# Gathering token rows by a slot-to-token map in a mixture of experts, with three products of rounded halves

## What is computed

```python
x = x3.reshape(-1, h)                       # 800 tokens, h = 256
probs = jax.nn.softmax(x @ Wg, axis=-1)     # 8 experts
vals, idx = jax.lax.top_k(probs, 2)
weights = vals / (jnp.sum(vals, axis=-1, keepdims=True) + EPS)
cw = zeros((T, E)).at[arange(T)[:, None], idx].set(weights)
act = silu(einsum('th,ehf->tef', x, W1) + b1)        # f = 1024
y = einsum('tef,efh->teh', act, W2) + b2
out = einsum('te,teh->th', cw, y)
shared = silu(x @ Ws1 + bs1) @ Ws2 + bs2
out = out + 0.1 * shared
```

## Time and profile before

| What | us |
|---|---|
| Median of 3 runs | 1086.58 (1086.11 to 1089.01) |
| The profiled execution | 1087.61 |
| Its span, first to last instruction | 1085.5 |
| Mean granted TensorE clock | 0.958 of full speed |
| PE busy | 992.4 (91%) |
| DVE busy | 809.2 (75%) |
| ACT busy | 748.4 (69%) |
| POOL busy | 626.2 (58%) |

### The profile page before, as it was taken

The page is one execution under the profiler, slowest core; times in us unless marked ns, Lnnn a source line. Parts: engine busy times, 40 slices in busy tenths (PEclk is TensorE's granted clock), DMA queues, the critical chain, the costliest instruction groups (busy, mean ns, idle before and its releaser), DMA issues.

```text
span 1085.5 us, 16818 instructions
## 1 busy us (share of the span) xinstructions
PE 992.4 (91%) x5808; PEld 688.4 (63%) x5808; DVE 809.2 (75%) x954; ACT 748.4 (69%) x1722; POOL 626.2 (58%) x388
## 2 busy tenths in 40 slices
PE   5994898988999999899998998898999899999996
PEld 3543555655656556565665666676777665899995
DVE  7797999999999999999999998577666630211110
ACT  4999998999999999999999932556556532233221
POOL 2001999999999999999999956311110005022122
PEclk9995899999999999999999999799899899999998
DMA  5001344444444434344444414501000009599994
GB/s 194 9 8 51 102 112 113 109 112 111 113 112 109 112 110 113 112 110 113 107 112 111 112 38 143 149 15 29 2 2 2 1 1 365 152 292 320 319 304 123
DMA packets 91118, 125.44 MB, mean 116 GB/s; under 512 B 11641, under 2 KB 84490, under 8 KB 91018
## 3 DMA queue, kind: packets, MB, share of 16 engines
q1 hardware_dynamic: 87130, 120.04, 38.6%
q0 software_dynamic: 3904, 4.33, 2.1%
HBM read 115.93 MB, written 9.23 MB: 115 GB/s over the span
## 4 chain that ended last, share of the span: by engine, by line
PE 49%; DVE 28%; issue 12%; ACT 6%; DMA 2%; POOL 1%; DVEq 0%; POOLq 0%; ACTq 0%
DVE states L1791 15%; PE ps L1233 14%; PE ps L1580 7%; PE ps L1594 6%; DVE states L1769 4%; PE ps L1213 4%; PE ps L1108 3%; PE ps L1366 3%; PE ps L1378 2%; PE ps L1125 2%; DVE neg_max L1907 2%; ACT probs L1030 2%; POOL rows_by_slot L796 1%; PE ps L1394 1%; PE ps L1515 1%
## 5 line engine op out<-in xcount | busy, mean ns | idle before, releaser
L705 POOL TENSOR_TENSOR states<-states,c_row 128x800 f32<-128x800 f32 x255 | 472.8, 1900 | 89.6 <-DVE states L1791 89.4
L1233 PE MATMUL ps<-states,ident 128*128 128x400 f32 x1024 | 381.1, 508 | 11.4 <-DVE u L1799 11.4
L1233 PEld LDWEIGHTS ps<-states,ident 128*128 128x128 f32 x1024 | 186.9, 192 | 116.7 <-DVE u L1799 12.7
L1791 DVE TENSOR_TENSOR_SCAN states<-sb_decay,ps 128x800 f32<-128x800 f32 x128 | 231.5, 1808 | 4.8 <-ACT sb_decay L944 3.9
L1791 DVE TENSOR_TENSOR_SCAN states<-ps,states 128x800 f32<-128x800 f32 x128 | 229.8, 1795 | 1.1 <-ACT ps L944 1.1
L936 ACT ACTIVATE xT<-xn_tok,xT 100x256 f32<-100x256 f32 x512 | 216.4, 493 | 0.7 <-PE ps L1213 0.2
L944 ACT ACTIVATE ps<-dt,neg_a 128x396 f32<-128x396 f32 x256 | 141.2, 583 | 45.1 <-DVE states L1791 44.2
L1213 PEld LDWEIGHTS ps<-ident,xT 100*128 100x128 f32 x1024 | 101.1, 145 | 81.2 <-issue 62.6
L944 ACT ACTIVATE sb_decay<-dt,neg_a 128x396 f32<-128x396 f32 x256 | 144.4, 611 | 1.0 <-DVE states L1791 0.9
L1213 PE MATMUL ps<-ident,xT 100*128 100x100 f32 x1024 | 114.9, 257 | 29.4 <-DVE states L1791 17.6
L1030 ACT ACTIVATE probs<-ps,neg_max 100x361 f32<-100x361 f32 x128 | 70.8, 560 | 65.0 <-DVE neg_max L1907 64.5
(11 more groups left out here) (233 smaller groups left out, 1258.7 us busy)
## 6 DMA issues: line engine op xcount, KB each, us to landing
c_row<-rows SPq DMA_DIRECT2D x256, 200.0 KB, 3.1
w_tile<-in_w SPq DMA_DIRECT2D x40, 1024.0 KB, 8.0
b_row<-rows SPq DMA_DIRECT2D x32, 200.0 KB, 3.1
ctx<-in_ctxT SPq DMA_DIRECT2D x8, 361.0 KB, 4.2
rows_by_slot<-blank_rows SPq DMA_DIRECT2D x1, 2660.0 KB, 11.6
x_tile<-rows_by_slot SPq DMA_DIRECT2D x20, 133.0 KB, 3.3
win<-in_winT SPq DMA_DIRECT2D x2, 1024.0 KB, 10.8
w_shared<-in_w SPq DMA_DIRECT2D x2, 1024.0 KB, 6.8
```

Of the source, the lines that this page charges most:

```text
L705: nc.gpsimd.tensor_tensor(st, st, c_row[i % C_SLOTS][:].unsqueeze(1).broadcast_to([P, CP, TQ]), ALU.mult).then_inc(product_ready, 1)
L1233: mm = nc.tensor.matmul(ps[:, j, 0:TQ], ident[:], states[i % RING][:, j * TQ:(j + 1) * TQ], start=(n == 0), stop=(n == N - 1), skip_group_ ...
L1791: nc.vector.tensor_tensor_scan(st, rates, inflows, 0.0, ALU.mult, ALU.add).then_inc(scan_done, 1)
```

## The change

Rows by a map. DVE no longer sends slots to POOL. `places` (new) turns each pick's slot into a one-hot tile (20 columns) and a one-hot place (128 columns) in bf16, and `tokens` on PE, at unit 10, multiplies them in 16 matmuls of 40 columns, so that each slot receives the number of its token. `token_numbers` on DVE turns the sums into indices (blank slots get the numbers of blank rows). The token rows, without the number, are stored in DRAM once, by one plain DMA (`token_rows`), and POOL gathers each tile's 128 rows from it with one indirect DMA (`fetch`): two after unit 12, three after the shared expert, and from there one behind each addition. The 16 scatters, their blank rows and SP's `load_rows` go; the waits of SP's weight loads stay, but the second load waits for the split of the second weights instead of `tile_done`.

Three products. The shared expert's weights are split by POOL during the attention (two passes for each of two 128x2048 blocks, ahead of the third context's split). The inputs are split by ACT and DVE (first half) and ACT and POOL (second half), the hidden values by ACT (rounded copy) and POOL (what is left) in four slots. For the tiles, ACT makes the rounded copy of the hidden values in two halves and of the second weights (`high_second`), and DVE makes the low parts (`low_hid`, `low_second`). The tiles' first product stays float32.

Ranks. The picks' sum, the counting matrices and the ones are bf16, and `ranks` comes at unit 5. DVE computes the owners of the tiles (`experts_ready`) before the slots.

The diff, cut:

```diff
-SECOND_HALF_AT, LOGITS_AT, RANKS_AT, ROWS_AT = 1, 2, 6, 13
+SECOND_HALF_AT, LOGITS_AT, SPLIT_AT, RANKS_AT, INVERT_AT, FETCH_AT, ROWS_AT = 1, 2, 3, 5, 10, 12, 13
-SHARED_LAG = 2
-ROUTE_CONSTS = 13
+SHARED_LAG, HIDDEN_SLOTS, FETCHED_EARLY = 2, 4, 2
+ROUTE_CONSTS = 16
@@ sp
                 if turn > 0:
-                    sp.wait_ge(tile_done, turn)
+                    sp.wait_ge(second_split, turn)
                 load_second(w_tile[r], e, w2_in[r])
-            def load_rows(k):
...
-                    sp.wait_ge(tile_added, 16 * (k - X_SLOTS + 1))
-                sp.dma_start(x_tile[r][:], rows_by_slot[k * P:(k + 1) * P]).then_inc(rows_in[r], 16)
+            sp.wait_ge(cw_ready, 1)
+            sp.wait_ge(xn_ready, (1 + DIRS + 2) * B)
+            sp.dma_start(token_rows[FIRST_ROW:FIRST_ROW + T].rearrange("(b l) w -> l b w", l=L), rows_src[:]
+                         ).then_inc(token_rows_stored, 16)
@@ pool
+            for n, cols in enumerate((slice(W1_AT, W2_AT), slice(W2_AT, B1_AT))):
+                split_into([part[:, cols] for part in shared_part], shared_raw[:, cols], shared_split, 2 * n)
             split_context(2, 0, 2)
...
-            for j in range(PICKS):
-                for b in range(B):
-                    at = bass.IndirectOffsetOnAxis(ap=slot_idx[:, j * B + b:j * B + b + 1], axis=0)
-                    nc.gpsimd.indirect_dma_start(rows_by_slot, at, rows_src[:, b, :], None).then_inc(scattered, 16)
+            def low_hidden(u):
+                high, low = hidden_part[u % HIDDEN_SLOTS]
+                pool.wait_ge(hidden_high, u + 1)
+                nc.gpsimd.tensor_tensor(low[:], hidden_raw[u % HIDDEN_SLOTS][:], high[:].bitcast(F32), ALU.subtract
+                                        ).then_inc(hidden_split, 1)
...
+            def fetch(k):
+                r = k % X_SLOTS
+                if k >= X_SLOTS:
+                    pool.wait_ge(tile_taken, k - X_SLOTS + 1)
+                    pool.wait_ge(tile_weighed, k - X_SLOTS + 1)
+                at = bass.IndirectOffsetOnAxis(ap=token_of[:, k:k + 1], axis=0)
+                nc.gpsimd.indirect_dma_start(x_tile[r][:], None, token_rows, at).then_inc(rows_in[r], 16)
+            for u in range(UNITS):
+                low_hidden(u)
+                if u == SPLIT_AT:
+                    for k in range(KD):
+                        low_inputs(k)
+                if u == FETCH_AT:
...
+                    for k in range(FETCHED_EARLY):
+                        fetch(k)
...
                 nc.gpsimd.indirect_dma_start(sums, at, y_tile[k % 2][:], None, compute_op=ALU.add
                                              ).then_inc(tile_added, 16)
+                if k + X_SLOTS < TILES:
+                    fetch(k + X_SLOTS)
@@ act, a shared unit
+                nc.scalar.activation(raw[:], ps[:, u % 2, 0:TQ], ACT.Silu,
+                                     bias=b1_shared[:, ft:ft + 1]).then_inc(silu_done, 1)
+                act.wait_ge(silu_done, u + 1)
+                nc.scalar.activation(hidden_part[u % HIDDEN_SLOTS][0][:], raw[:], ACT.Copy).then_inc(hidden_high, 1)
@@ act, a tile
+            def high_second(k):
+                act.wait_ge(w2_in[k % W_SLOTS], 16 * (k // W_SLOTS + 1))
...
+                    act.wait_ge(tile_done, k - 1)
+                nc.scalar.activation(second_part[k % 2][0], w_tile[k % W_SLOTS][:, W2_AT:B1_AT], ACT.Copy
+                                     ).then_inc(second_high, 1)
...
+                    if ft % 4 == 3:
+                        half = slice(ft - 3, ft + 1)
+                        act.wait_ge(tile_silu, FT * k + ft + 1)
+                        nc.scalar.activation(high[:, half, :], raw[:, half, :], ACT.Copy).then_inc(hid_high, 1)
+                if k + 1 < TILES:
+                    high_second(k + 1)
@@ pe
+            def tokens():
+                pe.wait_ge(places_ready, 1)
+                for j in range(PICKS * B):
+                    mm = nc.tensor.matmul(ps[:, TOKEN_BANK, 0:2 * TILES], hot_place[:, j, :], by_tile[:, j, :],
+                                          start=(j == 0), stop=(j == PICKS * B - 1))
...
             def shared_second(u):
-                pe.wait_ge(silu_done, u + 1)
+                pe.wait_ge(hidden_split, u + 1)
                 for m in range(KD):
...
+                    mm = three(ps[:, 4 + 2 * q + m, 0:TQ], [part[:, at:at + P] for part in shared_part],
+                               [part[:] for part in hidden_part[u % HIDDEN_SLOTS]], ft == 0, False)
@@ pe, out_of_tile
-                pe.wait_ge(w2_in[k % W_SLOTS], 16 * (k // W_SLOTS + 1))
+                pe.wait_ge(second_split, k + 1)
                 for ft in range(FT):
+                    if ft % 4 == 0:
+                        pe.wait_ge(hid_split, 2 * k + ft // 4 + 1)
+                    mm = three(ps[:, 6 + k % 2, 0:D], [part[:, ft, :] for part in hid_part[k % 2]],
+                               [part[:, ft * D:(ft + 1) * D] for part in second_part[k % 2]], ft == 0, ft == FT - 1)
@@ dve
+            def places():
+                picked = PICKS * B
+                step(nc.vector.tensor_tensor(hot_tile[:], slot_sum[:].unsqueeze(2).broadcast_to([L, picked, TILES]),
...
+                nc.vector.tensor_tensor(hot_place[:], place_in[:].unsqueeze(2).broadcast_to([L, picked, P]),
+                                        place_no[:].unsqueeze(1).broadcast_to([L, picked, P]), ALU.is_equal
+                                        ).then_inc(places_ready, 1)
...
+            def low_hid(k, half):
+                dve.wait_ge(hid_high, 2 * k + half + 1)
...
+            def low_second(k):
+                dve.wait_ge(second_high, k + 1)
+                high, low = second_part[k % 2]
+                nc.vector.tensor_tensor(low, w_tile[k % W_SLOTS][:, W2_AT:B1_AT], high.bitcast(F32), ALU.subtract
+                                        ).then_inc(second_split, 1)
...
             for k in range(TILES):
+                for half in range(2):
+                    low_hid(k, half)
                 if k + 2 < TILES:
                     take_tile(k + 2)
+                if k + 1 < TILES:
+                    low_second(k + 1)
                 weigh_tile(k)
```

More of the change, by code:

```diff
@@ L311, in decoder_layer, with in_place @@
         moe = ExitStack()
[L312 removed]
+        def in_place(name, shape):
+            with ExitStack() as first:
+                raw = sb(f"{name}_raw", shape, scope=first)
+            return raw, sb(f"{name}_low", shape, F32R, scope=moe)
+        shared_raw, shared_low = in_place("shared", [P, B1_AT])
+        b1_shared = sb("b1_shared", [P, FT], scope=moe)
         rows_src = sb("rows_src", [L, B, RW], scope=moe)
@@ L716, in split_into @@
                 high, low = part
-                nc.gpsimd.tensor_tensor(high, raw, one[:].unsqueeze(2).broadcast_to(raw.shape), ALU.mult
-                                        ).then_inc(done, 1)
+                ones_of = one[:].unsqueeze(2) if len(raw.shape) == 3 else one[:]
+                nc.gpsimd.tensor_tensor(high, raw, ones_of.broadcast_to(raw.shape), ALU.mult).then_inc(done, 1)
                 pool.wait_ge(done, count + 1)
@@ L1060, in _ @@
             for k in range(KD):
+                job_result(act, ("xn3T", k, 0))
+                nc.scalar.activation(xn3_part[0][:, k, chunk(0)], bank(("xn3T", k, 0))[:, 0:TQ], ACT.Copy
+                                     ).then_inc(xn3_high, 1)
+            for k in range(KD):
+                act.wait_ge(xn3_low[0], k + 1)
                 copy_out(("xn3T", k, 0), xn3T[:, k, chunk(0)], bank(("xn3T", k, 0))[:, 0:TQ])
@@ L1072, in _ @@
                     nc.scalar.activation(route["exp"][:], route["shifted"][:], ACT.Exp).then_inc(exp_ready, 1)
+                if u == SPLIT_AT:
+                    for k in range(KD):
+                        job_copied(act, ("xn3T", k, 1))
+                        nc.scalar.activation(xn3_part[0][:, k, chunk(1)], xn3T[:, k, chunk(1)], ACT.Copy
+                                             ).then_inc(xn3_high, 1)
                 if u == ROWS_AT:
@@ L1508, in shared_first @@
                 if ft == 0:
-                    for k in range(KD):
-                        job_copied(pe, ("xn3T", k, q))
-                if u >= 2:
+                    pe.wait_ge(xn3_low[q], KD)
+                if u < KD:
+                    job_copied(pe, ("xn3T", u, 0))
+                else:
                     pe.wait_ge(silu_done, u - 1)
                 for k in range(KD):
-                    mm = nc.tensor.matmul(ps[:, u % 2, 0:TQ],
-                                          w_shared[:, W1_AT + k * F + ft * P:W1_AT + k * F + (ft + 1) * P],
-                                          xn3T[:, k, chunk(q)], start=(k == 0), stop=(k == KD - 1))
+                    at = W1_AT + k * F + ft * P
+                    mm = three(ps[:, u % 2, 0:TQ], [part[:, at:at + P] for part in shared_part],
```

(5 more changed lines are left out.)

196 lines of the change are left out of this document (132 added, 64 removed).

## The result

The changed kernel takes 1078.7 us (median of five, 1072.01 to 1080.1) beside 1088.5 us for the kernel before in the same comparison: 0.9899, with a 95% interval from 0.9879 to 0.9918. It is 9.8 us faster; the prediction said 1071, 15.8 us less by its sum.

The account below looks back on a forecast made before the run. PE was taken to bound the tile loop, with additions already slower but hidden. 1087.6 - 9.2 (shared stage) - 12.6 (tiles) + 1.5 (loop's end) + 4.5 (additions) = 1071.8, median 1.0 lower: 1071 us; range 1058 to 1085.

Parts of the forecast that it names:

- Three products: Products of rounded halves replacing float32 ones: 7.4 us saved in the shared stage, 12.6 us in the tile loop.
- Ranks: Shared stage: ranks lose half their passes, 16 `tokens` matmuls bring as many short ones back; together 0 us.
- the part on the additions: Tile loop: additions at 7.51 us a step against PE's 6.62 delay it from tile 9; 4.5 us given back.
- the signs it gave: Expected in the loop's profile: PE's second-half idle time from DVE's low parts; a granted clock below 1.00 would be wrong.
- The slow clock: First `into_tile` after the shared stage: 5.08 us falls to 3.57 once the wait for rows goes; 1.5 us saved.
- the stage's sum: Shared stage: 7.4 + 0.8 + 1.5 - 0.5 = 9.2 us saved.
- The cover on POOL: Attention: splitting shared weights makes the third context's split 4.5 us late, hidden by 6.55 us of idle time; costs nothing.
- the 4.5 us charged for them: Tile loop: `low_hid(k + 1)` queues on DVE behind the weighing that waits for an addition; five tiles at 0.89 us.
- The 1.5 us at the loop's end: End of tile loop: `weigh_tile` (0.50), the first low part (0.63) and their waits are not hidden; 1.5 us lost.
- the one at 1078: Shared stage or ACT stretched, by ACT's load, a late gather or POOL's low parts: 6 to 8 us; chance 0.15.
- PE keeps the pace: Tile loop: additions step at up to 6.6 us, so the 4.5 us don't arise: 1066 us; chance 0.28.
- The rival on the other side: Tile loop: additions get slower, through DVE's low parts: 1076 to 1086 us (chance 0.07) or 1096 us (chance 0.10).

Follow-up runs that it names:

- the undoing: Ranks' products back on float32 ones and flags, against the changed kernel with the gather issued ahead of the addition (1069.98 us): 1073.2 us.
- the second profile of the changed kernel: The changed kernel, unaltered, measured and profiled once more: 1076.66 us (1072.06 to 1079.75, six times); the profile is that of the shortest time.

## Where the prediction was right, and where it failed

**Direction and range** were right; the time was some 7 us too low, and the step that failed is one sentence of the part on the additions. Of the signs it gave, two came out against it: PE's idle time in the loop is put down to gathers and not to DVE's low parts, and the granted clock there is 0.96 beside PE's gaps.

**Three products.** Their pitch is as taken. PE's timeline in the changed kernel:

```profile
924.73 0.28 PE L1229 MATMUL ps<-shared_high,hid_low 128*128 128x256 f32 x1
924.85 0.28 PE L1229 MATMUL ps<-shared_high,hid_h 128*128 128x256 f32 x1
```

0.12 us apart, and 36 products of 400 columns took 6.67 us (0.185 each; 0.184 was taken). A tile costs PE 6.65 us (6.62). In the shared stage the three products were worth 6.7 us by the medians; up to the first turned tile, with about the same mean clock in both (0.95 and 0.94), the float32 stage ran from 869.36 to 924.76 us and the changed one from 865.96 to 913.69, which is 7.7 us (7.4).

**Ranks** were the mis-sized term of the stage, set at nothing with the token sums. In the kernel before, 14 products stand ahead of the 16 in 1.80 us:

```profile
887.58 1.19 PE ps L1489 x14
```

In bf16 both together take 0.50 us, and the 16 products that `tokens` adds 0.41. So ranks and token sums together are worth 2.1 us by these rows; the 3.2 us of the undoing hold some slow clock that the kernel before didn't have. "As many short ones" was counted in products and not in time.

**The slow clock** behind the stage was to go with its cause, the wait for rows: 1.5 us gained. In the two profiles of the changed kernel it went. In the seven others with the same shared stage the wait is gone too, and the clock falls nevertheless, earlier and for longer, 3.3 us. So 1.5 us gained became 1.8 us lost there, 3.3 us off, for which the ranks made up in part: by the medians of one comparison all but the tiles' products brought 1088.15 - 1080.21 = 7.9 us, against 9.2 predicted. That the stage's sum came out near is luck: two terms were off, in opposite directions.

**The cover on POOL** held. Its timeline in the attention (in brackets idle time before), where the earlier trace rows had 6.55 us:

```profile
698.69 4.56 POOL L758 TENSOR_TENSOR shared_low<-shared_raw,shared_high 128x2048 fp32r<-128x2048 f32 x1
703.21 1.39 POOL L756 TENSOR_TENSOR ctx_h<-ctx,one 128x722 fp32r<-128x722 f32 x1
704.67 1.61 POOL L758 TENSOR_TENSOR ctx_l<-ctx,ctx_h 128x722 fp32r<-128x722 f32 x1
709.20 1.39 POOL L756 TENSOR_TENSOR ctx_h<-ctx,one 128x722 fp32r<-128x722 f32 x1 [2.92 <-PE ps L1229]
```

The third context's split is 3.6 us late and 2.9 us of room are left. The shared stage starts at 865.96 us here, at 866.08 before, and at up to 871.00 in the other profiles; it starts at 869.36 in the kernel that doesn't split the shared weights, so the spread is there without this split too.

**The additions** were read rightly, as far as they go: 7.76 us a step (7.51) while weights are loaded, until tile 14, and 4.3 to 5.2 us afterwards. But the 4.5 us charged for them were to come through a queue on DVE, and with that queue out of the way nothing changed (1077.42). The 1.5 us at the loop's end stand in the list of waits as 1.3 us. The sentence that failed: "A `fetch` stands behind each addition on POOL; its issue ... fits into the 5 us of waiting for the landing." It priced the issue alone. What had to be followed is when the issue may begin (after the landing of the addition before), when the rows land (7.2 us later, not the 4.7 of the row load), and when PE wants them. Rows had waited for additions before, too: SP loaded those of tile 15 when addition 10 had landed.

```profile
1017.05 1.54 POOL L805 DMA_INDIRECT sums<-y_tile,x_tile  x1 [5.66 <-DMA sums<-y_tile,x_tile]
1023.91 0.33 SPq L632 DMA_DIRECT2D x_tile<-rows_by_slot  x1
```

With 3.2 us to landing (the median of these loads) they were there some 10.1 us after the addition's issue, and PE turned them after 14.3 (1031.37). In the changed kernel they are there after 9.4 us (1007.47 to 1016.87), no later, but PE wants them after 7.3: with the additions 7.76 us apart and 6.65 us of PE's work a tile, it comes 1.1 us nearer to them with every tile. The prediction reckoned this room out for the queue on DVE and not for the rows. By the run with six buffers the late rows cost 5.8 us: of the tiles' 12.6 us 2.1 were left. With the gathers ahead of the additions, which also shortens the additions' steps, it is 10.2.

Among the rivals, the one at 1078 had "a gather lands late" in its list; it was right by that condition, though the place was the tile loop and not the stage. That its number was right is luck, for it was added up from 0.4 us a tile or a unit. The number of *PE keeps the pace*, 1066, is near what the kernel does once gathers and low halves are ahead (1067.3), but its condition doesn't hold there: the additions are 7.08 us apart up to tile 14, not 6.6.

**The rival on the other side**, additions slowed by DVE's low parts, shows in small. From 941 to 1035 us, POOL's groups in the changed kernel (busy us, mean ns of one):

```profile
L872 POOL DMA_INDIRECT sums<-y_tile,token_of x12 | 23.4, 1954 | 47.0 <-DVE y_tile L2261 34.0 <-DMA sums<-y_tile,token_of 13.0
L850 POOL DMA_INDIRECT x_tile<-token_rows,token_of x13 | 18.7, 1438 | 4.0 <-issue 3.4 <-DVE x_turned L2249 0.6
```

and with the tiles in float32, where DVE has no low parts:

```profile
L872 POOL DMA_INDIRECT sums<-y_tile,token_of x13 | 20.6, 1583 | 59.6 <-DMA sums<-y_tile,token_of 59.6
L850 POOL DMA_INDIRECT x_tile<-token_rows,token_of x13 | 12.9, 993 | 4.0 <-issue 3.7 <-DVE x_turned L2243 0.3
```

(The 34.0 us that the view puts down to `y_tile` are landings as well: each addition's own tile was weighed long before, and the next tile's `y_tile` waits for the same landing.) An issue is 0.4 us longer beside the low parts. In the kernel without weight loads, whose DVE has the same low parts, a gather's issue takes 0.99 us too, so it depends on whether the two meet. The longest one, 3.47 us at 951.88, runs beside a low part of 2.28 us that began at 951.61, and ends 1.5 us after it. The rule of the Trainium skill that the prediction weighed ("SBUF — State Buffer", section "SBUF: two separate sides") agrees with this; the price is 0.4 us of the addition's issue in a step of 7.8, not the 1.25 us that would have taken the whole gain.

## What to carry to other kernels

When a transfer moves to another engine's queue, its price is not the issue but the chain: what the issue now stands behind, how long the transfer takes under the traffic of that stage, and how far ahead of its use that leaves it. Five buffers were a lead of 5 us here (1009.67 to 1014.76), less than the 7.2 us to landing, because the issue of the fifth waited for the landing of an addition. When the engine that uses the rows gets faster, this room is to be reckoned out again. Put what only needs a free buffer ahead of what waits for a landing; that was one moved line and 7 to 8 us.

## What the runs showed of the hardware

- A gather of 128 rows that POOL issues lands in 2.8 us without the weight loads (DMA share 0.26) and in 7.2 us beside them (5.5 us in the kernel with the tiles in float32); an accumulating one in 4.1 us, and in 6.4 beside the loads in the kernel with the tiles in float32.
- PE's clock falls to half after a wait of 2.2 us in an otherwise full loop, so that the wait costs 3.7 us; after one of 1.7 us, in the second profile of the changed kernel, the 24 products behind it took 2.84 us, as usual. After 915 us it fell in seven profiles and not in two with the same shared stage, and also where PE had no halt ahead of it.
- Where POOL makes low parts beside it, an operation of DVE with two SBUF inputs is stretched. The operation of 2048 columns that makes the one-hot places, in the changed kernel:

```profile
889.09 3.02 DVE L2205 TENSOR_TENSOR hot_place<-place_in,place_no 100x2048 bf16<-100x2048 f32 x1
```

and in the kernel with the shared expert in float32, where POOL has none:

```profile
894.21 2.29 DVE L2189 TENSOR_TENSOR hot_place<-place_in,place_no 100x2048 bf16<-100x2048 f32 x1
```

It cost nothing, as the token numbers were ready (895.3 us) long before POOL came to the first gather (901.3 us).
